# Grouping the causal masks of cross-attention's score blocks in a decoder-layer kernel

## Chip, cores and metric

The kernel runs on one core of one Trainium2 chip. The metric is the device time of one execution in microseconds (us). The kernel before had a median of 1645.51 us over 3 runs (1641.98 to 1650.18).

## The reference, cut to what matters

One decoder layer over x of shape (8, 512, 256): a linear-attention block, then causal cross-attention against a context of the same shape, then a mixture of experts (16 experts, 4 per token, 512 hidden). The change lies in the scores of the cross-attention, with 16 heads of 64 columns:

```python
qh = (q @ Wq.T + bq).reshape(b, s, H, HD).transpose(0, 2, 1, 3)
kh = (k @ Wk.T + bk).reshape(b, s, H, HD).transpose(0, 2, 1, 3)
scores = jnp.einsum('bhqd,bhkd->bhqk', qh, kh) / np.sqrt(HD)
scores = jnp.where(jnp.tril(jnp.ones((s, s), bool)), scores, -jnp.inf)
attn = jax.nn.softmax(scores, axis=-1)
```

## The kernel before, in words

The program has three stages one behind the other: the first attention (to about 213 us of the profiled span), the heads of the cross-attention (to about 1112 us), and the experts. In the heads stage the loop runs over 8 batches of 8 **pairs** of heads, 64 pairs in all. A pair's two heads lie in partitions 0 to 63 and 64 to 127 of q and k, so that their matmuls contract over 64 rows each, in the two halves of the array ("64*128" in the rows), side by side.

The 512 queries of a head are four rows of 128, i = 0 to 3. Row i has (i + 1) x 128 allowed columns, of which the last 128 are the diagonal square that needs the mask. They are done in three **blocks**: block 3 (row 3, 512 columns), block 2 (row 2, 384 columns) and block 1 (rows 1 and 0, 256 and 128 columns; row 0 is computed 256 wide, `MIN_COLS`). Each block's scores go to two PSUM banks, one per head (`odd`), and two such pairs of banks (`slot`) are used in turn. The step `scores` (from line 1254) does a block on PE:
- it waits for q and k, and for the exponentials (`s_exp`) of the block that had its banks before (line 1262);
- for each row it issues three product terms of two matmuls (one per head), line 1269. The terms are high and low parts of q and k, float32 at full matmul rate (`split3`);
- then the row's mask, line 1274: an identity times a triangle of -1e30 in bf16, added to the diagonal square. It is split by its 128 contracted rows into two halves of 64, and per half there is a matmul for each head. The first half is 128 columns wide, the second 64 (its first 64 columns are zeros and skipped). So a mask is four matmuls, and a pair of heads has 4 masks, 16 mask matmuls;
- the block's last two matmuls give the signal `s_pe`.

DVE then takes the negated maximum of each row (line 1526), ACT the exponential with its sum (line 1400), and DVE scales the result by the inverse sum (line 1538, signal `s_norm`). PE transposes the probabilities (step `turn`, line 1286: 20 transposes of 128 x 128, after a wait for the pair's last `s_norm`), ACT copies them to SBUF (lines 1411 and 1414), PE multiplies them with V (step `weigh`, line 1298). In the same pairs PE projects k, q and v of what comes (lines 1240 and 1251), makes output products (line 1315) and routing (line 1331), through four work banks used in turn.

The order is written out by hand in `attention_plan` (line 981), and every engine goes through the same list of steps. For pair n it is, in short: scores of block 3, scores of block 2, the transposes of pair n - 1, the softmax steps of blocks 3 and 2, projections of pair n + 1, scores of block 1, its softmax, `weigh` of pair n - 1. Line 1026 has the first part, in which the two blocks stand back to back:

```python
plan += [("scores", (n, 3)), ("scores", (n, 2)), *start, *turns[0:2], ...
```

Of the kernel before, what the change touches and what calls it, by code (L numbers as in the profile page):

```python
# [15 lines left out]
P = 128  # L16
# [3 lines left out]
H, HD = 16, 64  # L20
# [242 lines left out]
def split3(a, b):  # L263
    (ah, al), (bh, bl) = a, b
    return ((al, bh), (ah, bl), (ah, bh))
# [682 lines left out]
ROWS_OF = {3: (3,), 2: (2,), 1: (1, 0)}  # L948
PROB_AT = {3: 0, 2: 512, 1: 896, 0: 1152}
SCORE_COL = {3: 0, 2: 0, 1: 0, 0: 256}  # L950
MIN_COLS = 256
# [97 lines left out]
def cross_attention(nc, sems, spent, d, x1_dram, x1_stored, out, rows_dram, routing, W, projecting, ahead, kept, hold, plan):  # L1049

    with ExitStack() as stack:
        p = Phase(nc, stack, sems, "xa")
# [8 lines left out]
        ident_of, mask_of, tri, onesb = ahead.ident_of, ahead.mask_of, ahead.tri, ahead.onesb  # L1061
# [15 lines left out]
        lg, repl, mask, key = small("lg"), small("repl", E + 4), small("mask"), small("key")  # L1077
# [25 lines left out]
        SB = [p.banks(f"S{i}", 2) for i in range(2)]  # L1103
# [104 lines left out]
        def tensor(pe, w, step, at):  # L1208
# [17 lines left out]
            elif step in ("project_k", "project_q"):  # L1226
                n = at
# [26 lines left out]
            elif step == "scores":  # L1254
# [2 lines left out]
                w.wait_ge(q_lo, n)  # L1257
                w.wait_ge(k_hi, n)
                w.wait_ge(k_lo, n)
                if at in before_in_slot:  # L1260
                    w.wait_ge(s_exp, (*before_in_slot[at], 1))
                bank_pair = SB[slot[at]]
                for i in ROWS_OF[blk]:
                    col, width = SCORE_COL[i], (i + 1) * P
                    n_cols = max(width, MIN_COLS)
                    for term, (qq, kk) in enumerate(split3(q[n % 2], k[n % 2])):
                        for odd in range(2):
                            mine = slice(HD * odd, HD * odd + HD)
                            pe.matmul(bank_pair[:, odd, col:col + n_cols], qq[mine, i * P:(i + 1) * P], kk[mine, 0:n_cols],  # L1269
                                      start=(term == 0), stop=False)  # L1270
                    for half in range(2):
                        for odd in range(2):
                            mine, skipped = slice(HD * odd, HD * odd + HD), HD * half
                            m = pe.matmul(bank_pair[:, odd, col + width - P + skipped:col + width], ident_of[mine, half, :],  # L1274
                                          mask_of[mine, half, skipped:P], start=False, stop=(half == 1))
                            if half == 1 and i == ROWS_OF[blk][-1]:
                                m.then_inc(s_pe.of((n, blk, odd)), 1)
            elif step == "turn":
                n, turn = at
                w.wait_ge(s_norm, (n, 1))  # L1280
# [785 lines left out]
```

## Time and profile before

| what | value |
|---|---|
| median of 3 runs (lowest, highest) | 1645.51 us (1641.98, 1650.18) |
| profiled execution, span from first to last instruction | 1636.8 us (its time outside the span isn't given) |
| PE busy | 1574.4 us, 96% |
| DVE busy | 1164.3 us, 71% |
| ACT busy | 1077.0 us, 66% |
| instructions | 35892 |

The span is the time from the first to the last instruction that the profiler recorded, in one execution. Busy is the time in which an engine has at least one instruction under way. On PE the instructions overlap: a matmul's duration holds its way through the array, in which the next one already streams. So what a matmul costs is read from the distance of two starts. PEld is the loading of weights, beside the matmuls. An instruction's line (L1274) is that of the code above.

### The profile page before, as it was taken

To read this page: it belongs to the slowest core of one execution; us is meant where nothing else is said; L and a number is where in the kernel's file an instruction comes from. 1 tells how busy PE (TensorE), PEld (TensorE's weight loads), DVE (VectorE), ACT (ScalarE), POOL (GpSimd) and SP (SyncE) were. 2 spreads that over 40 slices of the span, in tenths; PEclk is the share of its full clock that TensorE was granted. 3 is DMA by queue.
4 is the path that set the end of the run, shared out by engine and by line. 5 is a ranking of instruction groups with operands and counts; after the bars stand their busy time and mean duration, and the time that the engine had idled before them with its cause. 6 is when DMAs were issued, how large, how long until landed. Compare 5 with 4: busy or idle time off the path is not lost.

```text
span 1636.8 us, 35892 instructions
## 1 busy us (share of the span) xinstructions
PE 1574.4 (96%) x12438; PEld 1329.4 (81%) x12438; DVE 1164.3 (71%) x2745; ACT 1077.0 (66%) x2702; POOL 524.1 (32%) x440
## 2 busy tenths in 40 slices
PE   5999989999999999999999999997999999999997
PEld 4888867777777777777777777776999999999997
DVE  6877767676767677677677777777886666666663
ACT  3555557666766676676676667666776677677675
POOL 3444400000310300301202102104567745655655
PEclk9999999999999999999999999999999999999999
DMA  3122194044292490580730302046778887777874
GB/s 102 39 90 78 40 267 127 1 130 144 72 286 67 143 272 11 174 250 18 227 111 36 101 1 80 15 136 205 162 182 206 200 200 173 175 181 171 176 180 49
DMA packets 164610, 216.14 MB, mean 132 GB/s; under 512 B 16672, under 2 KB 124752, under 8 KB 164432
## 3 DMA queue, kind: packets, MB, share of 16 engines
q1 hardware_dynamic: 134080, 173.77, 35.2%
q0 software_dynamic: 28896, 38.62, 12.7%
q8 instruction: 103, 1.69, 0.4%
q10 hardware_dynamic: 1456, 1.44, 0.3%
q14 instruction: 75, 0.61, 0.1%
HBM read 90.76 MB, written 123.03 MB: 131 GB/s over the span
## 4 chain that ended last, share of the span: by engine, by line
PE 69%; ACT 14%; DVE 11%; issue 4%; DMA 1%; POOL 0%; SPq 0%; DVEq 0%; ACTq 0%
PE ex_H L1836 14%; PE ex_Y L1850 13%; ACT xa_prob L1400 7%; PE xa_work L1315 6%; PE xa_work L1240 5%; PE xa_work L1298 5%; PE xa_S L1269 5%; PE xa_work L1286 5%; PE xa_work L1251 4%; ACT xa_probT L1414 4%; PE a_work L458 4%; PE ex_X L1818 2%; DVE xa_nmax L1526 2%; DVE xa_prob L1538 2%; ACT xa_probT L1411 1%
## 5 line engine op out<-in xcount | busy, mean ns | idle before, releaser
L1400 ACT ACTIVATE xa_prob<-xa_S,xa_nmax 128x512 f32<-128x512 f32 (+3 forms) x512 | 265.9, 534 | 115.2 <-DVE xa_nmax L1526 97.6
L1943 POOL DMA_INDIRECT out<-ex_y,ahead_bits x158 | 272.8, 1727 | 200.7 <-POOLq L1939 73.6
L1836 PE MATMUL ex_H<-ex_xT,ex_w 128*128 128x256 f32 x1896 | 245.8, 286 | 5.9 <-issue 3.2
L1836 PEld LDWEIGHTS ex_H<-ex_xT,ex_w 128*128 128x128 f32 x1896 | 231.5, 191 | 6.8 <-issue 6.7
L1850 PE MATMUL ex_Y<-experts_w_hi,ex_hT 128*128 x1264 | 236.6, 280 | 0.2 <-issue 0.2
L1526 DVE TENSOR_REDUCE xa_nmax<-xa_S 128x2 f32<-128x1024 f32 (+3 forms) x256 | 198.1, 816 | 4.7 <-PE xa_S L1274 4.7
L1850 PEld LDWEIGHTS ex_Y<-experts_w_hi,ex_hT 128*128 128x128 f32 x1264 | 198.7, 188 | 0.5 <-issue 0.5
L1711 POOL DMA_INDIRECT expert_rows<-kept_xn,kept_rows x112 | 111.1, 992 | 266.6 <-DVE xa_prob L1538 224.2
L1921 DVE TENSOR_TENSOR ex_hT<-ex_h,ex_hT 128x512 fp32r<-128x512 f32 x158 | 108.2, 692 | 120.4 <-ACT ex_hT L1875 116.6
L1414 ACT ACTIVATE xa_probT<-xa_work 128x512 f32<-128x512 f32 x256 | 139.6, 603 | 81.9 <-PE xa_work L1286 73.4
L1850 PE MATMUL ex_Y<-experts_w_lo,ex_hT 128*128 x632 | 176.3, 279 | 0.0
L1538 DVE TENSOR_SCALAR xa_prob<-xa_prob,xa_sums 128x512 f32<-128x512 f32 (+3 forms) x512 | 169.3, 384 | 6.8
L1870 ACT ACTIVATE ex_h<-ex_H,kept_b 128x256 f32<-128x256 f32 x316 | 131.2, 466 | 63.6 <-DVE kept_b L1909 47.8
L1286 PE MATMUL xa_work<-ahead_ident,xa_prob 128*128 128x128 f32 x1280 | 155.4, 277 | 8.5 <-DVE xa_prob L1538 7.1
L1298 PE MATMUL xa_work<-xa_probT,xa_v 128*64 128x512 f32 (+3 forms) x1024 | 153.5, 442 | 2.2 <-ACT xa_probT L1411 2.2
L1286 PEld LDWEIGHTS xa_work<-ahead_ident,xa_prob 128*128 128x128 f32 x1280 | 139.4, 142 | 15.8 <-DVE xa_prob L1538 10.2
L1298 PEld LDWEIGHTS xa_work<-xa_probT,xa_v 128*64 128x64 f32 x1024 | 68.2, 137 | 82.9 <-issue 67.0
L1883 ACT ACTIVATE ex_y<-ex_Y,ahead_bits 128x256 f32<-128x256 f32 x158 | 73.9, 473 | 77.4 <-PE ex_Y L1850 57.0
L1533 DVE RECIPROCAL xa_sums<-xa_sums 128x2 f32<-128x2 f32 (+1 forms) x192 | 32.1, 167 | 128.4 <-ACT xa_prob L1400 128.3
L1850 PEld LDWEIGHTS ex_Y<-experts_w_lo,ex_hT 128*128 128x128 f32 x632 | 118.6, 188 | 0.0
L1400 ACT ACTIVATION_READ_ACCUMULATOR xa_prob<-xa_S,xa_nmax 128x1 f32 x512 | 108.8, 213 | 0.0
L1875 ACT ACTIVATE ex_hT<-ex_h 128x512 fp32r<-128x512 f32 x158 | 99.9, 632 | 5.0
(384 smaller groups left out, 3587.6 us busy)
## 6 DMA issues: line engine op xcount, KB each, us to landing
expert_rows<-xa_room_of_w_hi_and SPq DMA_DIRECT2D x256, 273.0 KB
kept_x<-expert_rows SPq DMA_DIRECT2D x52, 273.0 KB
ex_w_raw<-in_w SPq DMA_DIRECT2D x27, 512.0 KB
ahead_ctx<-in_w SPq DMA_DIRECT2D x26, 512.0 KB
ahead_x<-in_w SPq DMA_DIRECT2D x26, 512.0 KB
kept_xn<-expert_rows SPq DMA_DIRECT2D x27, 273.0 KB
experts_w_lo<-in_w SPq DMA_DIRECT2D x6, 1024.0 KB, 5.5
expert_rows<-xa_room_of_w_hi_and SPq DMA_DIRECT2D x32, 136.5 KB
```

What stands on the lines that cost most here:

```text
L1286: m = pe.transpose(PJ[:, col:col + P], prob[n % 2][:, odd, PROB_AT[i] + j * P:PROB_AT[i] + (j + 1) * P], ident[:])
L1298: m = pe.matmul(OB[HD * odd:HD * odd + HD, j * P:512], v[n % 2][:, j, first_col + HD * odd:first_col + HD * odd + HD], probT[:, odd, PROB_ ...
L1400: m = act.activation(prob[n % 2][:, odd, PROB_AT[i]:PROB_AT[i] + width], SB[slot[at]][:, odd, col:col + width], ACT.Exp, bias=nmax[n % 2][ ...
L1414: act.activation(probT[:, odd, first_col:first_col + 512], bank(step, at)[:], ACT.Copy).then_inc(t_ev.of(at), 1)
L1526: m = dve.tensor_reduce(nmax[n % 2][:, i, :], SB[slot[at]][:, :, SCORE_COL[i]:SCORE_COL[i] + (i + 1) * P], AX.X, ALU.max, negate=True)
L1538: m = dve.tensor_scalar(part, part, sums[n % 2][:, i, odd:odd + 1], None, ALU.mult)
L1711: pool.indirect_dma_start(rows_dram, bass.IndirectOffsetOnAxis(rows_i[b % 2][:, t, k:k + 1], 0), xn3[:, t, :], None).then_inc(scattered[of ...
L1836: m = pe.matmul(bank[:, (f % 2) * ROWS:(f % 2 + 1) * ROWS], ww[:, c, f * P:(f + 1) * P], xx[:, c, :], start=(i == 0), stop=(i == len(terms ...
L1850: m = pe.matmul(YB[a][:, 0:D], hh[:, f, a * P:(a + 1) * P], W2[:, bass.ds(own * WE + f * D, D)], start=(i == 0), stop=(i == len(terms) - 1))
L1870: i = act.activation(h32[:, f, :], HB[2 * (j % 2) + u][:, (f % 2) * ROWS:(f % 2 + 1) * ROWS], ACT.Gelu, bias=b1[j % 2][:, f:f + 1])
L1921: dve.tensor_tensor(hT[j % 2][1][:, fs, :], h32[:, fs, :], f32(hT[j % 2][0][:, fs, :]), op=ALU.subtract).then_inc(h_lo.of((j, u)), 1)
L1943: pool.indirect_dma_start(out, bass.IndirectOffsetOnAxis(tail[j % NT][:, a, 0:1].bitcast(I32), 0), y[j % NY][:, a, :], None, compute_op=AL ...
```

## The change

For blocks 3 and 2, block 2's mask is issued ahead of block 2's products, behind block 3's mask, and opens the bank (`start=True`). Block 2's products then add to it, and its last product gives the signal. The wait for block 2's banks moves along, to between the two masks. In block 1 the two rows' products are issued one behind the other, with `start` on the first alone, and one mask of two diagonal squares follows. Its four matmuls have 2 x 128 and 2 x 64 columns: the moving operand is the same triangle read twice, and the output has two runs. A pair then has 12 mask matmuls for 16, in two groups for four.

```diff
--- before.py
+++ after.py
@@ -1257,24 +1257,47 @@
                 w.wait_ge(q_lo, n)
                 w.wait_ge(k_hi, n)
                 w.wait_ge(k_lo, n)
-                if at in before_in_slot:
-                    w.wait_ge(s_exp, (*before_in_slot[at], 1))
                 bank_pair = SB[slot[at]]
-                for i in ROWS_OF[blk]:
-                    col, width = SCORE_COL[i], (i + 1) * P
-                    n_cols = max(width, MIN_COLS)
-                    for term, (qq, kk) in enumerate(split3(q[n % 2], k[n % 2])):
-                        for odd in range(2):
-                            mine = slice(HD * odd, HD * odd + HD)
-                            pe.matmul(bank_pair[:, odd, col:col + n_cols], qq[mine, i * P:(i + 1) * P], kk[mine, 0:n_cols],
-                                      start=(term == 0), stop=False)
+
+                def free(at_):
+                    if at_ in before_in_slot:
+                        w.wait_ge(s_exp, (*before_in_slot[at_], 1))
+
+                def products(masked):
+                    for i in ROWS_OF[blk]:
+                        col, width = SCORE_COL[i], (i + 1) * P
+                        n_cols = max(width, MIN_COLS)
+                        for term, (qq, kk) in enumerate(split3(q[n % 2], k[n % 2])):
+                            for odd in range(2):
+                                mine, last = slice(HD * odd, HD * odd + HD), masked and term == 2
+                                m = pe.matmul(bank_pair[:, odd, col:col + n_cols], qq[mine, i * P:(i + 1) * P], kk[mine, 0:n_cols],
+                                              start=(term == 0 and i == ROWS_OF[blk][0] and not masked), stop=last, skip_group_check=True)
+                                if last:
+                                    m.then_inc(s_pe.of((n, blk, odd)), 1)
+
+                def masks(to, first_col, blocks_, first):
                     for half in range(2):
                         for odd in range(2):
                             mine, skipped = slice(HD * odd, HD * odd + HD), HD * half
-                            m = pe.matmul(bank_pair[:, odd, col + width - P + skipped:col + width], ident_of[mine, half, :],
-                                          mask_of[mine, half, skipped:P], start=False, stop=(half == 1))
-                            if half == 1 and i == ROWS_OF[blk][-1]:
-                                m.then_inc(s_pe.of((n, blk, odd)), 1)
+                            diagonal = SB[slot[n, to]][:, odd, first_col:first_col + blocks_ * P].rearrange("p (i c) -> p i c", c=P)
+                            mask = mask_of[mine, half, skipped:P].rearrange("p (i c) -> p i c", i=1).broadcast_to([HD, blocks_, P - skipped])
+                            m = pe.matmul(diagonal[:, :, skipped:P], ident_of[mine, half, :], mask, start=(first and half == 0),
+                                          stop=(not first and half == 1), skip_group_check=True)
+                            if half == 1 and not first:
+                                m.then_inc(s_pe.of((n, to, odd)), 1)
+
+                if blk == 3:
+                    free(at)
+                    products(masked=False)
+                    masks(3, 3 * P, 1, first=False)
+                    free((n, 2))
+                    masks(2, 2 * P, 1, first=True)
+                elif blk == 2:
+                    products(masked=True)
+                else:
+                    free(at)
+                    products(masked=False)
+                    masks(1, P, 2, first=False)
             elif step == "turn":
                 n, turn = at
                 w.wait_ge(s_norm, (n, 1))
```

## Rows read from the trace of the kernel before

**Rows 1.** The page's head and its first part: busy time of PE.

```profile
span 1636.8 us, 35892 instructions
...
PE 1574.4 (96%) x12438; PEld 1329.4 (81%) x12438; DVE 1164.3 (71%) x2745; ACT 1077.0 (66%) x2702; POOL 524.1 (32%) x440
```

**Rows 2.** Table by stage: length, then PE, PEld, DVE, ACT, POOL busy, PEclk, DMA.

```profile
213.00:1112.00 899.00, 880.79 (x7038) 665.25 (x7038) 651.70 (x1675) 606.35 (x1631) 125.04 (x124) 1.00 0.41 123
...
549.00:661.00 112.00, 111.06 (x882) 84.03 (x882) 81.42 (x214) 76.20 (x207) 19.11 (x19) 1.00 0.52 155
```

**Rows 3.** PE's waits, 549 to 661 us: total, times, longest.

```profile
PE xa_work L1286 <- DVE xa_prob L1538: 0.7, 2, 0.4
```

**Rows 4.** The chain of waits, around two stretches off PE: start, length, what.

```profile
579.77 0.46 ACT xa_probT L1414
...
587.17 1.02 DVE xa_nmax L1526 x2
...
590.19 1.02 DVE xa_prob L1538 x4
...
591.25 2.40 PE xa_work L1286 x20
...
637.94 0.46 ACT xa_probT L1414
```

**Rows 5.** Groups by line and form on PE: the small mask matmuls, whole span.

```profile
L1274 PE MATMUL xa_S<-ahead_bits 64*128 64x64 bf16 x512 | 50.5, 189 | 0.0
```

**Rows 6.** Timeline of PE, block 1 of a pair: start, length, what.

```profile
610.67 0.39 PE L1240 MATMUL xa_work<-ahead_xT_hi,WqT_hi 128*128 128x512 f32 x1
610.99 0.39 PE L1269 MATMUL xa_S<-xa_k0hi,xa_q0lo 64*128 64x256 f32 x2
611.21 0.29 PE L1269 MATMUL xa_S<-xa_k0lo,xa_q0hi 64*128 64x256 f32 x2
...
611.45 0.27 PE L1274 MATMUL xa_S<-ahead_bits 64*128 64x128 bf16 x4
611.55 0.38 PE L1269 MATMUL xa_S<-xa_k0hi,xa_q0lo 64*128 64x256 f32 x2
611.75 0.30 PE L1269 MATMUL xa_S<-xa_k0lo,xa_q0hi 64*128 64x256 f32 x2
...
611.99 0.28 PE L1274 MATMUL xa_S<-ahead_bits 64*128 64x128 bf16 x4
612.20 0.28 PE L1331 MATMUL xa_work<-ahead_rw,ahead_xn 128*128 128x16 f32 x1
```

**Rows 7.** Timeline of PE, blocks 3 and 2 of a pair.

```profile
603.17 0.40 PE L1269 MATMUL xa_S<-xa_k0lo,xa_q0hi 64*128 64x512 f32 x2
603.40 0.40 PE L1269 MATMUL xa_S<-xa_k0hi,xa_q0hi 64*128 64x512 f32 x2
603.64 0.26 PE L1274 MATMUL xa_S<-ahead_bits 64*128 64x128 bf16 x4
603.74 0.42 PE L1269 MATMUL xa_S<-xa_k0hi,xa_q0lo 64*128 64x384 f32 x2
604.00 0.34 PE L1269 MATMUL xa_S<-xa_k0lo,xa_q0hi 64*128 64x384 f32 x2
604.17 0.34 PE L1269 MATMUL xa_S<-xa_k0hi,xa_q0hi 64*128 64x384 f32 x2
...
604.54 0.33 PE L1286 MATMUL xa_work<-ahead_ident,xa_prob 128*128 128x128 f32 x1
```

**Rows 8.** The chain of waits: one pair's transposes.

```profile
604.61 2.34 PE xa_work L1286 x20
```

**Rows 9.** The chain: block 1's first products, first and last of 34.

```profile
287.84 0.55 PE xa_S L1269 x6
...
1068.24 0.55 PE xa_S L1269 x6
```

**Rows 10.** Timelines of DVE and PE, 648 to 649.2 us: scaling, then transposes.

```profile
647.99 1.01 DVE L1538 TENSOR_SCALAR xa_prob<-xa_prob,xa_sums 128x256 f32<-128x256 f32 x4
...
649.09 0.33 PE L1286 MATMUL xa_work<-ahead_ident,xa_prob 128*128 128x128 f32 x1
```

## The prediction

> **What bounds the kernel now.** I began with the busy shares of the whole page [rows 1]: PE is busy for 96% of the span, so PE is the first suspect. The table by stage [rows 2] narrows that, and shows the granted clock at 1.00 there, the higher of its two levels (2.4 GHz), so the clock is no part of the question. The heads stage, where the changed masks are, runs from 213 to 1112 us; the expert stage behind it has none of them. Inside it a stretch of a steady batch (all from the second to the seventh look alike) shows PE busy for 111.1 of 112.0 us, with DVE at 81 and ACT at 76. But a busy share does not say that PE sets the pace in every pair. The waits of one batch [rows 3] name two places where PE stands still before the transposes of line 1286 until DVE has scaled the probabilities, 0.7 us together. Small as they are, they mark the pairs in which the ACT and DVE work is as long as PE's. The chain of waits shows how much of the time that is: from 579.77 to 591.25 us it runs over ACT and DVE alone [rows 4], while PE works beside it, and then it comes back to PE. From 637.94 it leaves PE again. Between such stretches it is PE from end to end. So PE bounds some pairs and ACT with DVE the others, in turn, with very little slack between them.
>
> What the changed line costs on PE is read from starts, not from durations, because matmuls overlap: a 64-column mask matmul has a mean duration of 189 ns [rows 5], yet a whole group of four takes 0.10 us, from 611.45 to the next product at 611.55 [rows 6]. There each product term (two matmuls, one per head, side by side) follows the one before by 0.12 us, but the first term of the second row, right behind a mask group, takes 0.20 (611.55 to 611.75). The first term there pays about 0.08 us for a weight load that the short mask matmuls don't cover. The same is in the group of blocks 3 and 2 [rows 7]: 0.26 against 0.17 us for the first and second term of 384 columns.
>
> **The change, part by part.**
>
> *Block 1.* Before, from 610.99 to the next step at 612.20, 1.21 us [rows 6]: row 1's terms 0.22 + 0.12 + 0.12, its masks 0.10, row 0's terms 0.20 + 0.12 + 0.12, its masks with the way to the next step 0.21. After, row 0's terms stand right behind row 1's, so the mask group between them goes (0.10) and so does the uncovered load (0.08). The shared group at the end has four matmuls still, but twice the columns: 256 and 128 in place of 128 and 64. Two heads run side by side, so that is 192 more column times. A column costs 0.43 ns: a 512-column term takes 0.23 us (603.17 to 603.40 [rows 7]) and a 256-column term 0.12 (611.21 to 611.45 holds two [rows 6]), 0.11 us for 256 columns. 192 x 0.43 = 0.083 us. Sum: 0.10 + 0.08 - 0.08 = **0.10 us less on PE per pair**, 6.4 us over 64 pairs.
>
> The trace has no matmul whose moving operand is one tile read twice and whose output is in two runs. From below I bound its column at 0.43 ns (no extra price). From above: of the transposes of line 1286, 128 columns each, the chain gives twenty 2.34 us [rows 8], 0.117 us for one and 0.91 ns a column; at this price the 384 column times of the shared group cost 384 x (0.91 - 0.43) = 0.18 us more than I reckon. I take the lower value: the nearest row is the same mask with the same bf16 type, and the halves of a group start about 0.07 us apart for 128 columns (the last of four starts at 603.64 + 0.26 - 0.19 = 603.71 [rows 5, 7]). The row's 0.07 holds 0.055 of columns and little else.
>
> The Trainium skill, page "TensorE: Matmul & The Clock Gate", section "LDWEIGHTS (loading the stationary operand)", would give another price: a weight load of 128 columns takes about 107 ns. If each of a group's two rounds of loads cost that where the matmul is shorter, a group would take over 0.2 us, the gain would be some 0.2 us a pair, and the sum near 7 us in place of the one below. The 0.07 and 0.10 us above speak against it here: a bf16 load of this size is mostly hidden.
>
> *Blocks 3 and 2.* Block 2's four masks move from behind its products to ahead of them, behind block 3's masks. Nothing is removed. In the middle two groups stand together, +0.10 us, with one uncovered load behind them as before. At the end, from the last term at 604.17 to the transposes at 604.54 it was 0.37 us [rows 7]; without the masks it is the streaming of 384 columns (0.17) plus a switch from half-array to whole-array tiles. The nearest row for the switch is the opposite one, from the projection at 610.67 to the scores at 610.99: 0.32 for a 512-column matmul of 0.22, so 0.10. That makes 0.27, -0.10. Sum **zero**. Bounds: -0.03, if the second group's two halves cost their columns alone (128 + 64 by 0.43 ns is 0.08, less a little for the start-up that the last group now has at 603.64); +0.07, if the switch behind a float32 matmul must wait for the end of its duration of 0.34 us [rows 7] in place of 0.27. At the upper bound the 64 pairs lose 4.5 us and the gain of block 1 is mostly gone, 1644.
>
> *Waits.* Block 2's wait on the exponentials of the previous pair's block 1 now stands between the two mask groups. Before, it stood behind the same block-3 masks as the first thing of block 2. What is queued behind it is the same, and block 3's signal is given before it. Block 2's signal comes with its last product instead of its last mask, by the sum above at about the same time; block 1's comes some 0.1 us sooner after the start of its group. No DMA, ACT or DVE instruction is added, removed or moved, and no queue is passed.
>
> *What of it reaches the end.* A gain on PE counts only where the chain runs over PE. I counted the chain's pieces through the heads stage: 34 of the 64 block-1 groups lie on it, from the one at 287.84 to the one at 1068.24 [rows 9], five in each steady batch of eight, one in the first and three in the last. The others run beside ACT and DVE stretches such as [rows 4], whose length has nothing of line 1274 in it. One more pair is close: at 649.09 the transposes start 0.09 us behind DVE's end (647.99 + 1.01) [rows 10], against 0.04 where they truly wait (590.19 + 1.02 = 591.21, then 591.25 [rows 4]); its spare 0.05 is too small to take 0.10, and it is already off the chain. So 34 x 0.10 = **3.4 us**, with 0.2 for the groups of blocks 3 and 2, where the working above leaves some 5 ns each (0.10 in, 0.10 to 0.11 out). The profiled execution's span of 1636.8 us [rows 1] becomes 1633.2. The page gives no time of its own beside that span; the median of the runs is 8.7 us above it, the lowest run 5.2. I carry the difference, 3.6 us, to the median: 1645.5 - 3.6 = **1641.9 us**. What is late next is DVE's scaling before the transposes: the wait of [rows 3] grows by 0.1 us in each of its pairs.
>
> **The rivals.**
> 1. *PE's whole gain arrives.* If the ACT and DVE stretches are themselves started sooner, since block 1's scores are ready 0.1 us earlier, all 64 pairs count: 6.4 us, with the -0.03 bound of blocks 3 and 2 up to 8.3, so 1637.2 to 1639.1. For it: each of these stretches holds a maximum over block 1's scores, which can't start before PE has made them. Against it: in [rows 4] that maximum (587.17) comes behind DVE's own work, not behind PE. A removed group that is worth more than its 0.10 us would give the same time.
> 2. *Slower: the shared mask streams at the transposes' rate.* Place: the last four matmuls of block 1. At 0.91 ns a column a pair gets 0.18 - 0.10 = 0.08 us slower on PE, and the PE-bound pairs are then more than 34: between 34 and 64 x 0.08, +2.7 to +5.1, so 1648.2 to 1650.6. For it: a pattern never seen in this trace. Against it: the transposes are float32, the masks bf16. It decides once the group costs over 0.10 us more than columns say; over 0.5% slower needs 0.23 more in every pair. If the two heads' shared masks also ran one after the other, a further 0.35, it would be +15 or more.
> 3. *Nothing arrives.* The slack is used up by the first 0.04 us in the near-bound pairs, and five pairs a batch are too tight as well: 0 to -1.5 us, 1644 to 1645.5. For it: 0.04 and 0.09 are close together, and blocks 3 and 2 at their upper bound would do the same. Against it: the chain stays on PE without a break from 591.25 to 637.9, nearly half of a batch.
> 4. *The change isn't what it says:* the 192 added column times might swallow the removed group. They do nearly (0.083 against 0.10 us); only the uncovered load makes the gain. Were that load to reappear at row 0's first term, the gain is 0.02 x 34 = 0.7 us, within rival 3's time.
>
> **How the numbers follow.** Half a per cent, 8.2 us, is about what a measurement can tell from no change here; the three runs before already span 8.2 us. Chances: forecast (1640 to 1643.5) 0.52; whole gain 0.16; nothing, with 4, 0.20; slower 0.12. The centre is the forecast's 1641.9. The range takes in the whole gain and the slower case's first size, and some microseconds for the scatter of runs: 1634 to 1650. Faster by over 0.5% needs the whole gain at its upper end, or scatter on top of it: 0.13. Slower by over 0.5% needs rival 2's dearer form or scatter: 0.06. Within 0.5%: 0.81.
>
> **What would show it.** In the changed profile the 64-column mask matmuls should fall from 512 [rows 5] to 256. Block 1's stretch should go from 1.21 to 1.11 us, with row 0's first term at 0.12; blocks 3 and 2 together should keep their length (1.37 us from the second product term at 603.17 to the transposes at 604.54). The halves of the shared mask should start 0.12 us apart; 0.2 or more would prove rival 2. The wait of line 1286 on DVE should grow while the pairs it bounds keep their period. I am wrong if the period of a bound pair shrinks too (rival 1), or if block 1's stretch shortens and the batch does not (rival 3).

## The result, and the profile after

The changed kernel took **1633.1 us** (median of 4 runs, 1632.16 to 1635.61) against 1644.53 for the kernel before in the same session (4 runs, 1641.98 to 1650.18): a ratio of **0.9926, 95% interval 0.9905 to 0.9947**, faster by 0.7%. The forecast was 1641.9 us, the range ended at 1634.0, and "within 0.5%" had the chance 0.81. So the time lay outside the range, on the good side, and the gain was about three times the 3.6 us forecast.

Line numbers of the helpers move by up to 23: score products stand in L1273, masks in L1284, transposes in L1309, DVE's maximum in L1549, its scaling in L1561, GpSimd's indirect transfer in L1734.

The page's head and its first part, for [rows 1]:

```profile
span 1631.3 us, 35380 instructions
...
PE 1569.2 (96%) x12182; PEld 1319.9 (81%) x12182; DVE 1163.6 (71%) x2745; ACT 1077.6 (66%) x2702; POOL 520.0 (32%) x440
```

256 matmuls are gone, all of them 64-column masks, as forecast: 512 in [rows 5], 256 here. The groups of PE's masks by line and form (count, busy time, mean ns):

```profile
L1284 PE MATMUL xa_S<-ahead_bits 64*128 64x128 bf16 x384 | 35.8, 221 | 3.0 <-ACT xa_prob L1423 2.8
L1284 PE MATMUL xa_S<-ahead_bits 64*128 64x64 bf16 x256 | 18.9, 190 | 0.0
L1284 PE MATMUL xa_S<-ahead_bits 64*128 64x256 bf16 x128 | 18.3, 279 | 0.0
```

Block 1 of a pair, timeline of PE, for [rows 6]:

```profile
608.57 0.38 PE L1273 MATMUL xa_S<-xa_k0hi,xa_q0lo 64*128 64x256 f32 x2
608.79 0.28 PE L1273 MATMUL xa_S<-xa_k0lo,xa_q0hi 64*128 64x256 f32 x2
...
609.02 0.28 PE L1273 MATMUL xa_S<-xa_k0hi,xa_q0lo 64*128 64x256 f32 x2
609.14 0.28 PE L1273 MATMUL xa_S<-xa_k0lo,xa_q0hi 64*128 64x256 f32 x2
...
609.38 0.34 PE L1284 MATMUL xa_S<-ahead_bits 64*128 64x256 bf16 x4
609.65 1.40 PE L1354 MATMUL xa_work<-ahead_rw,ahead_xn 128*128 128x16 f32 x11
```

From 608.57 to 609.65 it is **1.08 us**, where 1.11 was forecast and 1.21 stood before. Row 0's first term (609.02 to 609.14) costs 0.12: the uncovered load is gone. The four shared masks are one row of 0.34 us, and the second half's matmuls, of 128 columns, last 0.22, so the halves start 0.12 us apart, as forecast for 256 columns. The end, masks with the way to the next step, grows from 0.21 to 0.27 us, by 0.06 where the forecast reckoned 0.08 for the added columns. Blocks 3 and 2, for [rows 7]:

```profile
600.63 0.40 PE L1273 MATMUL xa_S<-xa_k0lo,xa_q0hi 64*128 64x512 f32 x2
...
601.11 0.35 PE L1284 MATMUL xa_S<-ahead_bits 64*128 64x128 bf16 x8
...
601.73 0.34 PE L1273 MATMUL xa_S<-xa_k0hi,xa_q0hi 64*128 64x384 f32 x2
601.99 0.44 PE L1309 MATMUL xa_work<-ahead_ident,xa_prob 128*128 128x128 f32 x2
```

From 600.63 to 601.99 it is 1.36 us against 1.37: nothing, as forecast. The end is 0.26 (601.73 to 601.99), forecast 0.27.

**Where the time went.** Every pair has one group of transposes, so the distance from one pair's first transpose to the next pair's is the pair's period. I took these starts from the trace. One steady batch of each kernel, pair by pair, in us:

```
                 1      2      3      4      5      6      7      8
before, 561.2  17.93  12.17  13.29  13.55  19.15  11.85  13.04  12.83
after,  558.8  17.80  12.18  13.17  13.53  19.04  11.81  12.96  12.89
```

Pairs 1 to 7 give 100.98 before and 100.49 after: 0.49 less, 0.48 to 0.55 in each of the six steady batches, 3.1 us in all. With 0.07 in the first batch and 0.39 in the last it is **3.5 us, about the forecast's 3.4**. Pair 8 is different. Its six periods are

```
before   12.82  12.84  12.83  12.78  12.81  12.82   sum 76.90
after    12.20  12.18  12.89  12.17  12.91  12.17   sum 74.52
```

So 2.4 us more come from pair 8 alone, 0.6 to 0.7 us at a time or not at all, which no column of a mask explains. Together that is 5.9 us, the difference of the two heads stages (from the first transposes to the last pair's, 890.8 and 884.9 us). The rest of the difference between the medians (11.4 us) isn't in this pair of profiles at all: the profiled execution of the changed kernel took 1632.96 us, in the middle of its runs, and the first profile of the kernel before about 1638.5 (its span and the same 1.7 outside it), 3.5 us below its fastest timed run.

PE's waits in the same window as [rows 3] say it too. There were two, 0.36 us before the transposes of pair 1 and 0.30 before those of pair 3; now there is one:

```profile
PE xa_work L1309 <- DVE xa_prob L1561: 0.4, 1, 0.4
```

Pair 3's is 0.39, longer by the 0.1 us that was forecast. Pair 1's is gone after the batches in which pair 8 takes 12.2 us, and 0.39 where it takes 12.9. So this wait of PE hangs on what is late in pair 8.

**What is late in pair 8.** It shows in the chain of waits (start, length, what). Before, 669 us:

```profile
669.53 2.40 issue
671.93 1.73 ACT xa_prob L1400 x8
```

and in the timeline of the same place:

```profile
669.57 0.75 DVE L1519 SCALAR_TENSOR_TENSOR xa_q1lo<-xa_work,ahead_bqT,xa_q1hi 128x512 fp32r<-128x512 f32 x1 [0.37 <-ACT xa_q1hi L1385]
669.73 0.28 PE L1274 MATMUL xa_S<-ahead_bits 64*128 64x128 bf16 x4
670.43 0.96 POOL L1711 DMA_INDIRECT expert_rows<-kept_xn,kept_rows  x1 [0.30 <-issue]
670.87 0.69 DVE L1526 TENSOR_REDUCE xa_nmax<-xa_S 128x2 f32<-128x512 f32 x1 [0.56 <-PE xa_S L1274]
```

The last masks of block 1 end at 670.01 and DVE's other work at 670.32 (669.57 + 0.75), yet the maximum over block 1's scores starts at 670.87. The trace's semaphore events explain it: PE's two updates for the two heads are recorded at 670.13 and 670.85. In the pair's other groups, away from the transfers, the two updates are recorded 0.014 and 0.045 us behind the recorded ends of their matmuls. After, one batch of each kind. First the late one:

```profile
666.75 0.35 PE L1284 MATMUL xa_S<-ahead_bits 64*128 64x256 bf16 x4
667.63 0.96 POOL L1734 DMA_INDIRECT expert_rows<-kept_xn,kept_rows  x1 [0.30 <-issue]
668.14 0.69 DVE L1549 TENSOR_REDUCE xa_nmax<-xa_S 128x2 f32<-128x512 f32 x1 [0.62 <-PE xa_S L1284]
...
780.13 0.35 PE L1284 MATMUL xa_S<-ahead_bits 64*128 64x256 bf16 x4
780.15 0.75 DVE L1542 SCALAR_TENSOR_TENSOR xa_q1lo<-xa_work,ahead_bqT,xa_q1hi 128x512 fp32r<-128x512 f32 x1 [0.37 <-ACT xa_q1hi L1408]
780.81 0.68 DVE L1549 TENSOR_REDUCE xa_nmax<-xa_S 128x2 f32<-128x512 f32 x1
781.08 0.96 POOL L1734 DMA_INDIRECT expert_rows<-kept_xn,kept_rows  x1 [0.30 <-issue]
```

At 667.10 the masks end, the second update comes at 668.11 and DVE starts at 668.14, having stood 0.62 us. In the next batch the updates are there at 780.70 and 780.74, 0.24 and 0.26 us late themselves, but DVE's own work covers that, and it goes on without idle time (780.81). Pair 8 then costs 12.17 instead of 12.89 and the chain there holds PE alone:

```profile
780.29 0.18 PE xa_S L1284 x4
780.47 0.43 PE xa_work L1380 x2
```

GpSimd issues a row of indirect transfers there (the scatter of the expert rows), 0.96 us each, one every 1.27. The updates more than 0.4 us late, counted in the heads stage, are 20 of the masks' 384 before and 5 of their 256 after. Every one belongs to a matmul that ends during such a transfer or within 0.51 us of one, and the same holds for PE's other updates in the stage. In the first attention, where there are no transfers, none of some 150 is over 0.015 us late. That is a coincidence in one trace of each, so the experiments had to move one against the other.

### The profile page after: what moved, and what is told of

Its sections match the earlier page's. It is cut to its first block, busy times and chain, and to the rows that moved or that the text cites. A ratio compares the mean times of both kernels' runs of the same rounds, so it can differ in the third digit from the quotient of the medians.

```text
span 1631.3 us, 35380 instructions
## 1 busy us (share of the span) xinstructions
PE 1569.2 (96%) x12182; PEld 1319.9 (81%) x12182; DVE 1163.6 (71%) x2745; ACT 1077.6 (66%) x2702; POOL 520.0 (32%) x440
## 3 DMA queue, kind: packets, MB, share of 16 engines
q0 software_dynamic: 28896, 38.62, 12.9%
## 4 chain that ended last, share of the span: by engine, by line
PE 71%; ACT 13%; DVE 11%; issue 3%; DMA 1%; POOL 0%; SPq 0%; DVEq 0%; ACTq 0%; POOLq 0%
PE ex_H L1859 14%; PE ex_Y L1873 13%; PE xa_work L1240 6%; ACT xa_prob L1423 6%; PE xa_work L1338 6%; PE xa_S L1273 6%; PE xa_work L1309 5%; PE xa_work L1321 5%; PE xa_work L1251 4%; PE a_work L458 4%; ACT xa_probT L1437 3%; DVE xa_nmax L1549 2%; PE ex_X L1841 2%; DVE xa_prob L1561 2%; PE a_work L538 1%
## 5 line engine op out<-in xcount | busy, mean ns | idle before, releaser
L1966 POOL DMA_INDIRECT out<-ex_y,ahead_bits x158 | 268.4, 1699 | 205.1 <-ACT ex_y L1906 80.0
L1549 DVE TENSOR_REDUCE xa_nmax<-xa_S 128x2 f32<-128x1024 f32 (+3 forms) x256 | 197.7, 814 | 2.7 <-PE xa_S L1284 2.7
L1734 POOL DMA_INDIRECT expert_rows<-kept_xn,kept_rows x112 | 110.7, 988 | 262.5 <-DVE xa_prob L1561 220.2
L1561 DVE TENSOR_SCALAR xa_prob<-xa_prob,xa_sums 128x512 f32<-128x512 f32 (+3 forms) x512 | 169.4, 384 | 6.8
L1309 PE MATMUL xa_work<-ahead_ident,xa_prob 128*128 128x128 f32 x1280 | 157.2, 278 | 9.9 <-DVE xa_prob L1561 8.8
L1309 PEld LDWEIGHTS xa_work<-ahead_ident,xa_prob 128*128 128x128 f32 x1280 | 140.5, 142 | 28.9 <-DVE xa_prob L1561 19.3
```

Source lines behind the costliest of these rows:

```text
L1309: m = pe.transpose(PJ[:, col:col + P], prob[n % 2][:, odd, PROB_AT[i] + j * P:PROB_AT[i] + (j + 1) * P], ident[:])
L1549: m = dve.tensor_reduce(nmax[n % 2][:, i, :], SB[slot[at]][:, :, SCORE_COL[i]:SCORE_COL[i] + (i + 1) * P], AX.X, ALU.max, negate=True)
L1561: m = dve.tensor_scalar(part, part, sums[n % 2][:, i, odd:odd + 1], None, ALU.mult)
L1734: pool.indirect_dma_start(rows_dram, bass.IndirectOffsetOnAxis(rows_i[b % 2][:, t, k:k + 1], 0), xn3[:, t, :], None).then_inc(scattered[of ...
L1966: pool.indirect_dma_start(out, bass.IndirectOffsetOnAxis(tail[j % NT][:, a, 0:1].bitcast(I32), 0), y[j % NY][:, a, :], None, compute_op=AL ...
```

## The experiments

The theories: **A**, fewer PE instructions and nothing else (3.4 us); **B**, PE's completion signal of block 1 is held up by GpSimd's indirect transfers, and the change moves it out of their way; **C**, the profile of before was a favourable execution, and both kernels should be measured again.

**1. Both kernels again**, unchanged.

> The kernel before, unchanged, timed against itself, to see how far its executions scatter and whether its profile repeats. Both theories: ratio 1.000. Theory A (the whole difference is PE time of the masks): the pair whose transposes start near 434, 548, 662 us and so on takes 12.8 us in every batch, as in the profile before, since PE's work is the same. Theory B (a PE signal that falls beside GpSimd's indirect DMAs arrives late, and the change moved it): the same pair takes 12.2 us in some batches and 12.8 in others from execution to execution, or 12.8 in all; the runs scatter by several us.

> The changed kernel again. Theory A: about 5 us faster than before (the two spans, 1636.8 and 1631.3 us), and the 0.65 us that some batches gained in one pair are there in the same batches. Theory B: between 5 and 12 us faster, with 12.2 us for that pair in another number of batches than the four of the first profile.

Before: median 1645.46 us, ratio to itself 1.0007 [0.9994, 1.0021]. After: 1633.82, **0.9945 [0.9928, 0.9961]**. The gain is real: 9 to 12 us. So C is right about the profile but not about the gain. The second profile of the kernel before has a span of 1643.9 us, 7.1 more than the first one, of the same kernel. Its pair 8 takes 14.35, 12.87, 14.35, 12.87, 12.94 and 12.88 us (80.3 in all, 3.4 more than in the first profile; neither theory had named 14.35), and two other pairs were 1.35 and 1.7 us longer. The second of the changed kernel gives 12.18, 12.19, 12.90, 12.20, 12.18, 12.20. A pair 8 of 14.35, timeline of the kernel before:

```profile
444.15 0.96 POOL L1711 DMA_INDIRECT expert_rows<-kept_xn,kept_rows  x1 [0.30 <-issue]
444.71 0.28 PE L1274 MATMUL xa_S<-ahead_bits 64*128 64x128 bf16 x4
445.41 0.96 POOL L1711 DMA_INDIRECT expert_rows<-kept_xn,kept_rows  x1 [0.30 <-issue]
447.37 0.69 DVE L1526 TENSOR_REDUCE xa_nmax<-xa_S 128x2 f32<-128x512 f32 x1 [2.08 <-remote]
```

The masks end at 444.99; the updates are recorded at 446.63 and 447.34. Here the wait is 2.08 us, and "remote" is all the profile says of it: the second update comes 2.36 us behind its matmul's end, and the profile no longer matches the two. The same in the chain of waits, `another core or an unknown queue`:

```profile
444.54 0.75 DVE xa_q1lo L1519
445.29 2.05 another core or an unknown queue
...
447.37 1.03 DVE xa_nmax L1526 x2
```

**2. Half of the change each.** The first has the change in block 1 alone; the second has it in blocks 3 and 2 alone, block 1 as before.

```
# block 1 only
 if blk == 3:
     free(at)
     products(masked=False)
     masks(3, 3 * P, 1, first=False)
-    free((n, 2))
-    masks(2, 2 * P, 1, first=True)
 elif blk == 2:
-    products(masked=True)
+    free(at)
+    products(masked=False)
+    masks(2, 2 * P, 1, first=False)
# blocks 3 and 2 only
 else:
     free(at)
-    products(masked=False)
-    masks(1, P, 2, first=False)
+    (each row's products and its own four masks, as before)
```

> Block 1 grouped as in the change, blocks 3 and 2 as before. My sum: PE saves 0.10 us a pair here and nothing in blocks 3 and 2, so this kernel should have the whole PE gain, a bit over 3 us of the steady periods. Theory A: as fast as the changed kernel within 1 us. Theory B: as fast too if it is block 1's signal that matters, since it comes 0.1 to 0.2 us sooner after its group's start here as well; the late signal of block 1 (up to 1 us behind its mask) should be rarer than before.

> Blocks 3 and 2 as in the change, block 1 as before. My sum: zero, between +0.07 and -0.03 us a pair, so within 2 us of before. Theory A: the same as before, the pair near 662 us at 12.8 in all batches. Theory B: the same unless the moved signal of block 2 changes what it meets; a gain of over 3 us here would show that blocks 3 and 2 hold what the sum missed.

Block 1 only: 1636.26 us, **0.9951 [0.9933, 0.9969]**, and pair 8 at 12.18 or 12.19 in all six batches. Blocks 3 and 2 only: 1642.87, 0.9992 [0.9975, 1.0009], pair 8 at 14.35 once and 12.88 to 12.94 five times, and the other steady pairs within 0.04 us of before, 0.35 us less in the six batches together. Block 1 alone takes 2.2 us off pairs 1 to 7 of the six, where both halves take 3.1. So what the runs can tell from no change comes from block 1, pair 8's part too, and the other half is worth some tenths of a microsecond by the periods. By the medians block 1 alone is 2.4 us slower than the changed kernel, outside the 1 us expected, but the two ratios can't be told apart.

**3. The transfers moved away from pair 8's signal.** One of the scatter steps, issued behind block 2, goes behind block 1 of the same pair, in each of the kernels.

```
-SCATTER_AT = {..., 0: ((3, 3), (4, 2), (5, 1)), ...}
+SCATTER_AT = {..., 0: ((3, 3), (4, 1), (5, 1)), ...}
```

> The kernel before with two of GpSimd's indirect DMAs (part 4 of a batch's scatter) gated on the pair's block 1 instead of its block 2, so that block 1's mask signal of that pair no longer falls beside them. Theory A (only PE time of the masks counts): as before within 1 us, the pair at 12.8 us. Theory B (the signal is late beside the indirect DMAs): that pair goes from 12.8 (at times 14.4) to 12.2 us in all batches, 4 to 6 us faster than before, unless other signals now fall beside the moved DMAs.

> The changed kernel with the same two DMAs moved. Theory B: little gain over the changed kernel (0 to 2 us), since its signal already escapes in most batches; against the kernel before with the same edit it is then faster by the PE part alone, 3 to 4 us. Theory A: the difference between the two stays what it is without the edit, 9 to 11 us by the runs.

Pair 8 falls to 12.25 us in all six batches of the kernel before (73.5 us, where the second profile without the edit has 80.3 and the first 76.9), and to 12.18 to 12.20 in the changed one. The block's two updates are then no later than 0.05 us. That is what B says. But the time doesn't fall: 1648.47, 1.0017 [1.0003, 1.0031], and 1641.04, 0.9970 [0.9955, 0.9985]. The row of transfers now stands beside the next pair, whose period goes from 17.93 to 19.25, 19.43, 19.50, 21.22 and 20.89 us (in the changed kernel from 17.80 to between 18.97 and 21.13). There it is not only signals that are late. In the timeline of the kernel before with the moved step PE itself stands:

```profile
571.81 0.96 POOL L1711 DMA_INDIRECT expert_rows<-kept_xn,kept_rows  x1 [0.30 <-issue]
571.82 0.40 PE L1240 MATMUL xa_work<-ahead_xT_hi,WqT_hi 128*128 128x512 f32 x1
...
572.82 0.23 PE L1274 MATMUL xa_S<-ahead_bits 64*128 64x128 bf16 x1
573.51 0.21 PE L1274 MATMUL xa_S<-ahead_bits 64*128 64x128 bf16 x1 [0.34 <-issue]
574.22 0.21 PE L1274 MATMUL xa_S<-ahead_bits 64*128 64x64 bf16 x2 [0.49 <-issue]
574.45 0.69 ACT L1385 ACTIVATE xa_q0hi<-xa_work,ahead_bqT 128x512 fp32r<-128x512 f32 x1 [2.48 <-remote]
```

The projection ends at 572.22 (571.82 + 0.40) and ACT, which waits for it, starts at 574.45, while PE starts its next masks 0.7 us apart. A signal that doesn't get away seems to hold up what PE starts behind it. The delay is tied to the place of the transfers, and moving them only chooses whom it hits. Both theories missed the distance of the two kernels: it is 7.4 us by the medians, where B said 3 to 4 and A 9 to 11. In the profiles 2.3 us of it lie in the pair beside the moved transfers.

**4. One signal instead of two.** In the late cases the two updates of a group stand 0.7 us apart. If each has to be waited for, one for both heads should save 0.7 us.

```
-s_pe, s_exp = signal("s_pe", heads_of), ...
+s_pe, s_exp = signal("s_pe", [at for at in heads_of if at[2] == 1]), ...
-if half == 1 and i == ROWS_OF[blk][-1]:
+if half == 1 and odd == 1 and i == ROWS_OF[blk][-1]:
```

> The kernel before with one signal per block, from the second head's last matmul, in place of one from each head. In the profiles the two updates of a late pair come 0.7 us apart (670.13 and 670.85 us), DVE waiting for the second. Theory B: the pair drops by about 0.7 us to 12.2 us in most batches, 3 to 6 us faster than before. Theory A: no change, within 1 us, PE's work is the same.

> The changed kernel with one signal per block. Theory B: 0 to 2 us faster than the changed kernel, 12.2 us in all batches; against the kernel before with one signal only the PE part is left, 3 to 5 us. Theory A: the same as the changed kernel, and 9 to 11 us better than the kernel before with one signal.

It changes nothing: 1646.52, 1.0004 [0.999, 1.0017], and 1634.31, 0.9942 [0.9925, 0.9959]. Pair 8 has 12.86 to 14.33 in the one and 12.17 to 12.89 in the other, as without the edit. The number of updates is not what costs. That guess of mine fell.

**5. The same PE work added in two places.** Eight more masks on columns that nobody reads, in block 1 ahead of its shared group or in block 2 ahead of its products. PE's added work is the same 0.17 us a pair (block 1's record grows from 0.34 to 0.51, and block 2's stretch in the chain from 0.19 to 0.36), but only the first delays block 1's signal. Part of the computation is added here, none is left out.

```
# in block 1
+for _ in range(2):
+    masks(1, 3 * P, 1, first=False, signal=False)
 masks(1, P, 2, first=False)
# in block 2
+for _ in range(2):
+    masks(2, 3 * P, 1, first=False, signal=False)
 products(masked=True)
```

> The changed kernel with eight filler mask matmuls (two sets of 128 and 64 columns a head, into 128 columns that nobody reads) ahead of block 1's masks. PE does about 0.19 us more a pair, and block 1's signal comes 0.19 us later after the pair's transposes. Theory A (PE time alone): 34 to 40 pairs pay, 6 to 8 us slower than the changed kernel, the pair near 434, 547, 660 us stays at 12.2 us. Theory B (that signal's place against GpSimd's indirect DMAs): on top of it this pair goes back to 12.9 and at times 14.4 us in all or nearly all batches, so 10 to 14 us slower than the changed kernel, as slow as the kernel before or slower.

> The same eight filler matmuls, but in block 2's bank ahead of its products, so in front of the pair's transposes: PE does the same 0.19 us more a pair, and block 1's signal keeps its distance from the transposes. Theory A: as slow as the one with the filler in block 1, within 1 us. Theory B: the pair near 434 us stays at 12.2 us in most batches, so this kernel is 3 to 6 us faster than the one with the filler in block 1.

In block 1: 1652.88 us, **1.0047 [1.0030, 1.0063]**. In block 2: 1642.74, **0.9982 [0.9969, 0.9994]**. The same instructions cost 10.1 us more in the one place, where PE alone would make no difference. In the profiles the heads stages differ by 11.2 us. Pair 8 has 14.47, 14.31, 14.38, 14.36, 14.37, 14.32 in the first and 12.64, 12.67, 13.27, 12.67, 13.25, 12.67 in the second: 9.0 us of the 11.2. Mask updates over 0.4 us late were 22 in the first and 4 in the second. The direction is B's, the sizes are not: against the changed kernel the first is 19 us slower (10 to 14 expected), and in the second pair 8 doesn't stay at 12.2. There the added work brings the transposes' own signals beside a transfer: one that ends at 551.54 is recorded 0.76 us late, where the changed kernel has no transpose over 0.3 late. What that costs wasn't tried. With the work in block 1:

```profile
559.42 0.96 POOL L1736 DMA_INDIRECT expert_rows<-kept_xn,kept_rows  x1 [0.30 <-issue]
559.80 0.51 PE L1284 MATMUL xa_S<-ahead_bits 64*128 64x128 bf16 x12
560.69 0.96 POOL L1736 DMA_INDIRECT expert_rows<-kept_xn,kept_rows  x1 [0.30 <-issue]
562.61 1.02 DVE L1551 TENSOR_REDUCE xa_nmax<-xa_S 128x2 f32<-128x512 f32 x2 [2.04 <-remote]
```

and with it in block 2:

```profile
557.43 0.96 POOL L1736 DMA_INDIRECT expert_rows<-kept_xn,kept_rows  x1 [0.30 <-issue]
557.81 0.35 PE L1284 MATMUL xa_S<-ahead_bits 64*128 64x256 bf16 x4
558.50 1.01 DVE L1551 TENSOR_REDUCE xa_nmax<-xa_S 128x2 f32<-128x512 f32 x2
558.69 0.96 POOL L1736 DMA_INDIRECT expert_rows<-kept_xn,kept_rows  x1 [0.30 <-issue]
```

The cases that have been shown can be put in one row, by how long before the next transfer's start the masks end, and how long after their end DVE starts:

```
                              masks' end to transfer   to DVE's start
work added in block 1         0.38                     2.30
before, second profile        0.42                     2.38
before, first profile         0.42                     0.86
after, 667 us                 0.53                     1.04
work added in block 2         0.53                     0.34
after, 780 us                 0.61                     0.34
```

(The two 0.34 are DVE's own work before it.) Each row stands for one batch, and 0.53 stands in it with both outcomes. In the six steady batches of each profile but those of experiments 3 and 6 the order holds: where block 1 ended less than 0.52 us ahead of the next transfer, its second update was 0.78 to 2.4 us late every time (31 batches). Where it ended 0.52 to 0.61 ahead, with block 1 as changed, it was 1.0 us late in 7 of 29 and 0.2 to 0.3 in the others. So the 0.1 us by which the change ends the block sooner turn a delay in every batch into one in some.

**6. Block 1's shared mask ahead of its products**, so that it opens the bank and the signal hangs on the last product.

```
 else:
     free(at)
-    products(masked=False)
-    masks(1, P, 2, first=False)
+    masks(1, P, 2, first=True)
+    products(masked=True)
```

> The changed kernel with block 1's shared mask ahead of its products too, opening the bank, and the signal on the last product. PE's matmuls are the same. My sum: the mask's short matmuls then leave the first product's weight load uncovered (0.08 us), and the way from the last product to the next step is as long as from the mask. Theory A: 2 to 3 us slower than the changed kernel. Theory B: the signal comes about as late as with the filler of half its length, some batches return to 12.9 us, 3 to 6 us slower.

> The kernel with block 1's mask ahead of its products once more, since I had expected it 2 to 6 us slower than the changed kernel and it came out 2 us faster by the medians (1631.8 against 1633.8 us). If that is real, its ratio to the kernel before is again 0.991 to 0.994 and the steady pairs are again some 0.05 us shorter than with the mask behind; if it was the luck of few late signals, the steady pairs are as long as the changed kernel's and the ratio is 0.994 to 0.996.

I expected it to be slower and it wasn't: 1631.84 us, 0.9922 [0.9904, 0.9941], the lowest median on the chip of experiments 3 to 5. The profiled execution is the slowest of its six runs (1638.56). It loses its time behind the heads stage (525.5 us from the last pair's first transposes, where the changed kernel's two profiles have 518.9 and 520.1); the heads stage itself is 1.1 us shorter than in the first profile of the changed kernel. Pair 8 is 12.17 to 12.19 in four batches of six and 12.88 or 12.89 in two. Its block 1 takes 1.03 us (609.08 to 610.11), timeline of PE:

```profile
609.08 0.34 PE L1284 MATMUL xa_S<-ahead_bits 64*128 64x256 bf16 x4
609.22 0.37 PE L1273 MATMUL xa_S<-xa_k0hi,xa_q0lo 64*128 64x256 f32 x2
...
609.90 0.28 PE L1273 MATMUL xa_S<-xa_k0hi,xa_q0hi 64*128 64x256 f32 x2
610.11 1.06 PE L1354 MATMUL xa_work<-ahead_rw,ahead_xn 128*128 128x16 f32 x8
```

The 0.08 us for an uncovered load is there as I had summed it (the first product takes 0.20, 609.22 to 609.43), but in the other order the first product takes 0.22 as well, behind the projection, so nothing is added. Three of the steady pairs are 0.06 us shorter than with the change.

The second run, on another chip, took 1626.50 us, a ratio of 0.9950 [0.9932, 0.9968]; there the kernel before takes 1633.71 us, 12 less than on the first. Pairs 1 to 7 have the same periods. Pair 8 hasn't: it is 12.17 to 12.20 in all six batches. The transfers stand where they stood, and in this profile the signals aren't late. Timeline:

```profile
667.00 0.28 PE L1273 MATMUL xa_S<-xa_k0hi,xa_q0hi 64*128 64x256 f32 x2
...
667.67 0.68 DVE L1549 TENSOR_REDUCE xa_nmax<-xa_S 128x2 f32<-128x512 f32 x1
667.85 0.96 POOL L1734 DMA_INDIRECT expert_rows<-kept_xn,kept_rows  x1 [0.31 <-issue]
```

The last product ends 0.57 us ahead of the transfer, and its updates come 0.014 and 0.045 us behind it. At such a distance (0.58 to 0.66) the same kernel had the second of them 0.30 to 1.07 us late in its first run. In that whole profile no update of PE that can be matched to its matmul, 1434 in all, is over 0.053 us late; each of the other thirteen profiles has 15 to 47 over 0.4 in its heads stage. So the transfers alone don't make the delay: what else it takes, this chip doesn't have or didn't have then.

Of the two signs named ahead, the periods speak for a gain and the ratio for the luck of few late signals. By these intervals it can't be told from the change (0.9926 and 0.9945): the gain on PE is read from the trace, about 0.05 us a pair, and what it is worth at the end isn't measured.

## Why the prediction was wrong

- **What bounds the kernel, and what of PE's gain reaches the end: right in kind, and in size partly by luck.** The count of 34 of 64 pairs, from the chain of waits, gave 3.4 us, and pairs 1 to 7 gave 3.5. But a pair's PE saved 0.13 us, not 0.10, and 34 times that is 4.4. Of the five pairs counted in a batch (1, 3, 4, 5 and 7) three gave their full 0.11 to 0.13, pair 7 gave 0.08 and pair 4 only 0.02; pair 6, not counted, gave 0.04. Two errors cancel in the sum, and why pair 4 kept its length stays open. Pair 2, the one of [rows 4], kept its period (12.17 and 12.18). Rival 1 (all 64 pairs, 6.4 us) gives a sum near the 5.9 us between the first two profiles but not by its mechanism: pair 2 would have become shorter too. Rival 3 (nothing arrives) falls with the 3.5 us, rival 4's returning load with the 0.12 of row 0's first term.
- **Block 1 on PE: right**, 1.08 against 1.11; the two terms that go are as worked out, and the added columns cost 0.06 us in place of 0.08. **Rival 2** (the shared mask at the transposes' rate) is refuted by the 0.34 us of the record and by the 1.08. The estimate of 7 us from the 107 ns a load, by the section "LDWEIGHTS (loading the stationary operand)" of the Trainium skill's page "TensorE: Matmul & The Clock Gate", isn't borne out either: 0.13 us of PE is saved in a pair, not 0.2. **Blocks 3 and 2: right**, zero within 0.01 us a pair, and shown alone in experiment 2.
- **The step that failed is "Waits".** It said that block 1's signal "comes some 0.1 us sooner" and "no queue is passed", and put no price on it. No queue of instructions was passed, but a stream of GpSimd's transfers stands beside that signal in one pair of each batch. In the kernel before, it was late in every batch, by 0.8 to 0.95 us or by 2.4; 0.1 us sooner, it is mostly 0.2 to 0.3 late, which DVE's own work covers. Over four profiles each of kernels with block 1 as before (before twice, blocks 3 and 2 only, one signal) and with block 1 as changed (after twice, block 1 only, one signal), pair 8 takes 13.12 and 12.36 us on average: 0.76 x 6 = **4.6 us, more than the whole forecast**. I had the row that shows it, DVE's wait on the masks over the heads stage (total, times, longest): `DVE xa_nmax L1526 <- PE xa_S L1274: 4.7, 8, 1.2`. One of the eight is the 0.56 us above, when DVE's own work was over. And one of the two waits of [rows 3], pair 1's 0.36 us, came from it. I took the stretches over ACT and DVE for fixed in length, since [rows 4] shows one (587.17) in which the maximum waits for DVE alone; pair 8 is the one in which it waits for PE.
- **The second failed step is the one from the span to the median.** The median lay 8.7 us above the span, and I carried the difference of 3.6 across as if those 8.7 were the same in both kernels. Only 1.7 us of it stand outside the span. The other 7 were for the most part stalls that this one execution had not met and that others have: the second profile of before spans 1643.9, with 3.4 us more in pair 8 and 3.05 in two single pairs. The changed kernel has fewer of them, so its median lies close to its span (1.8 above).
- **The sum as it is now**: 3.5 on PE, 4.6 in pair 8, and one or two single stalls of 1.3 to 1.8 us which I found in the later profiles of before-like kernels (two in the second of the kernel before, one each in the blocks-3-and-2 and the one-signal kernels) and in none of the four profiles with block 1 as changed (that with work added in block 1 has one of 1.3 again). They come to 1.6 us a profile on average. That is 8 to 11 us; 9 to 12 were measured. The heads stages of the same two times four profiles say the same: 890.8, 897.7, 894.4 and 894.7 us with block 1 as before, 884.9, 884.4, 884.8 and 885.5 as changed, 9.5 less on average. What follows the last pair's first transposes is no part of it: 518 to 523 us in both kinds. The last part rests on four profiles of each kind and wasn't tried by itself.

**What stays open.** That the delay, where there is one, is tied to the nearness of PE's signal to GpSimd's indirect transfers is shown from both sides: by moving the transfers (experiment 3) and by moving the signal (experiment 5). What in the chip holds the signal back isn't: no trace shows its way. Nor is it shown why one of the three chips of the experiments has no late signal with the same transfers at the same places (experiment 6), so the 4.6 us can't be promised there. Open too is why pair 8 alternates between 12.2 and 12.9 from one batch to the next in the changed kernel; why in one pair of the second profile of the kernel before PE stood 1.7 us in the products of probabilities and values, with no transfer beside it; and how much of the 12 us by which that chip runs the kernel before faster comes from the missing late signals. The one profile on it has none, and behind the last pair's first transposes it takes 514.2 us, where the other thirteen take 518.2 to 525.8; there is no profile of the kernel before on it.

## What to carry to other kernels

When an engine waits for PE although PE's last instruction has long ended, compare the semaphore's time with the instruction's end before taking the stretch as fixed, and look at what GpSimd transfers there: a signal 0.1 us sooner or later was worth 0.7 or 2 us here, on two chips, and there was no late signal on another, so measure such a gain on more than one. Compare the profiled execution with the fastest run before making sums on it: when it lies below all of them, the runs hold stalls that it doesn't show, and a change may remove those as well. Work with no effect on the result, placed once ahead of the suspected signal and once elsewhere, tells a cost of place from a cost of work.

## What was not expected of the hardware

- PE's completion signal, normally 0.014 to 0.05 us behind its matmul, came up to 2.4 us late beside GpSimd's indirect transfers (0.96 us each, every 1.27), and up to 4.0 us in the kernel before with the moved step (a matmul that ends at 800.46, its update at 804.50). On one of the three chips of the experiments none was over 0.053 us late. In the same stretch PE's own next matmuls started 0.7 us apart in place of 0.1, without anything that they waited for in the profile. The profile names such a releaser "remote" or "another core or an unknown queue", on a program of one core.
- The mask ahead of its products took less than behind them. As the opening of the bank it is 0.14 us to the first product (609.08 to 609.22), but the end is 0.21 (609.90 to 610.11) where mask and end together took 0.27: 1.03 us in all against 1.08. The first product takes about as long in either place (0.20 and 0.22).
- A moving operand read twice, with its output in two runs, cost no more than its columns: 256 columns in a pair of matmuls took 0.12 us, the same as a float32 product of 256 (0.12).
